# Cross maxima handed over head by head, division and rounding of the outputs on GpSimd, and another order of VectorE's steps

## The reference, cut to what matters

```
x = layernorm(x + self_attention(x))      # 16 heads of 32, 8 key-value heads, rotary angles
x = layernorm(x + cross_attention(x, ctx))# 16 heads of 32, causal, keys and values of ctx @ Wkv
x = layernorm(x + ffn(x))                 # silu(x @ w1.T) * (x @ w2.T) @ w3.T

# self attention: all 4 blocks of 128 keys are among the 8 selected, so no key is masked
scores = q @ k.T / sqrt(32);  probs = softmax(scores);  out = (probs @ v) @ wo
# cross attention: scores = where(lower triangle, scores, lowest float)
# ffn weights go through NF4 and back: scaled = block / max|block| per 64 weights,
# the nearest of 16 steps, times the scaler, which is itself stored as 8 bits about its mean
```

## Time and profile before

| | before |
|---|---|
| median of 3 runs, us | 1255.36 (1251.58 to 1261.95) |
| profiled execution, us | 1259.52 |
| its span, us | 1257.6 |
| mean granted clock of TensorE | 0.935 |
| busy us: TensorE, VectorE, ScalarE, GpSimd | 1063.7, 793.3, 474.3, 396.2 |

### The profile page before, as it was taken

How to read it: one execution, slowest core, us unless ns; L and a number is a source line. 1 busy time by engine, 2 the same in 40 slices (tenths; PEclk the granted TensorE clock), 3 DMA queues, 4 the chain that set the end, 5 groups by cost and what they waited for, 6 DMA issues and landing times.

```text
span 1257.6 us, 17320 instructions
## 1 busy us (share of the span) xinstructions
PE 1063.7 (85%) x6248; PEld 681.6 (54%) x6248; DVE 793.3 (63%) x1628; ACT 474.3 (38%) x582; POOL 396.2 (32%) x427
## 2 busy tenths in 40 slices
PE   6869697888898789898887888878868899999995
PEld 4535244444554435445544555545534688888884
DVE  6676554765677466854876786687585554545444
ACT  3323242463444463453465455455434121212100
POOL 4526743384535634301223222222243600000000
PEclk9769898998998799999898998999897999999998
DMA  5722266355632674363475456457552510202010
GB/s 199 218 54 47 73 164 174 95 145 144 192 96 94 168 204 129 108 131 86 113 193 137 119 136 154 106 133 174 138 129 72 171 51 1 101 1 67 1 67 34
DMA packets 81808, 145.12 MB, mean 115 GB/s; under 512 B 14984, under 2 KB 31728, under 8 KB 81468
## 3 DMA queue, kind: packets, MB, share of 16 engines
q1 hardware_dynamic: 68812, 104.03, 32.1%
q0 software_dynamic: 11888, 39.73, 10.9%
q10 hardware_dynamic: 1024, 0.26, 0.1%
HBM read 78.09 MB, written 23.73 MB: 81 GB/s over the span
## 4 chain that ended last, share of the span: by engine, by line
PE 59%; DVE 20%; ACT 5%; POOL 5%; DMA 5%; issue 4%; SPq 1%; ACTq 0%; DVEq 0%; POOLq 0%
PE att_pv L922 11%; PE att_scores L1134 6%; PE att_pv L1134 6%; PE att_scores L866 6%; PE att_scores_T L1164 6%; PE att_scores_T L854 6%; PE att_scores_T L855 5%; PE att_scores_T L856 5%; PE att_scores_T L898 3%; DVE att_mx L1469 3%; DVE att_scores L1464 3%; ACT att_probs L1290 2%; PE att_scores_T L1024 2%; DMA att_q_stack<-att_m_rows 2%; DVE att_nf_zone L1586 2%
## 5 line engine op out<-in xcount | busy, mean ns | idle before, releaser
L1290 ACT ACTIVATE att_probs<-att_scores_T 128x1024 f32<-128x1024 f32 (+2 forms) x256 | 219.3, 883 | 311.6 <-PE att_scores_T L898 308.5
L866 PE MATMUL att_scores<-att_k_stack,att_q_stack 96*128 96x256 f32 (+1 forms) x504 | 166.2, 413 | 78.6 <-DVE att_mx L1469 49.4
L922 PE MATMUL att_pv<-att_probs,att_v 128*32 128x512 f32 (+3 forms) x1024 | 226.7, 568 | 5.3 <-POOL att_probs L708 4.9
L922 PE MATMUL att_pv<-att_probs,att_ones 128*32 128x512 f32 (+3 forms) x1024 | 226.7, 568 | 0.0
L1469 DVE TENSOR_REDUCE att_mx<-att_scores 128x2 f32<-128x1024 f32 x124 | 151.6, 1223 | 107.5 <-PE att_scores L866 106.6
L1464 DVE CUSTOM_DVE_ANT_0 att_scores<-att_scores,att_cmask 128x128 f32<-128x128 f32 (+3 forms) x256 | 120.9, 511 | 59.6 <-PE att_scores L866 59.0
L866 PEld LDWEIGHTS att_scores<-att_k_stack,att_q_stack 96*128 96x128 f32 x504 | 88.8, 203 | 124.2 <-DVE att_mx L1469 45.7
L898 PE MATMUL att_scores_T<-att_q_stack,att_k_stack 97*128 97x512 f32 (+2 forms) x512 | 146.3, 398 | 11.4 <-DVE att_nf_zone L1600 4.5
L708 POOL TENSOR_SCALAR_AFFINE_SELECT att_probs<-att_probs 128x256 f32<-128x256 f32 x128 | 59.6, 466 | 264.5 <-ACT att_probs L1290 262.3
L898 PEld LDWEIGHTS att_scores_T<-att_q_stack,att_k_stack 97*128 97x128 f32 x512 | 90.9, 201 | 56.7 <-issue 18.0
L922 PEld LDWEIGHTS att_pv<-att_probs,att_v 128*32 128x32 f32 x1024 | 51.9, 116 | 119.0 <-issue 94.8
(11 more groups left out here) (251 smaller groups left out, 2083.0 us busy)
## 6 DMA issues: line engine op xcount, KB each, us to landing
att_q_stack<-att_q_hi SPq DMA_DIRECT2D x128, 128.0 KB, 3.1
att_probs<-nf_x SPq DMA_DIRECT2D x28, 352.0 KB, 3.6
att_nf_home<-nf_reciprocals POOLq DMA_DIRECT2D x48, 176.0 KB, 5.0
att_q_stack<-att_q_lo SPq DMA_DIRECT2D x64, 128.0 KB, 3.6
att_k_stack<-att_k_hi SPq DMA_DIRECT2D x64, 128.0 KB, 3.5
att_nf_home<-nf_x SPq DMA_DIRECT2D x20, 352.0 KB, 3.6
w_nf<-att_nf_zone SPq DMA_DIRECT2D x192, 22.0 KB, 2.6
att_k_stack<-att_k_hi SPq DMA_DIRECT2D x64, 64.0 KB, 2.6
```

The source lines that it names most:

```text
L866: last = T.matmul(sco[:, r, 0:width], qst[0:96, s, r, P * t:P * t + P], kst[0:96, r if crossed(b) else 0, s, 0:width], start=True, stop=True)
L922: last = T.matmul(pv[HD * j:HD * j + HD, sums, q0:S], lhs, pr[:, at:at + S - q0], start=(t == 0), stop=(t == TT - 1))
L1290: A.activation(probs_of(b, r)[:, 1024 * h:1024 * h + w], bank[:, 0:w], ACT.Exp, scale=SCALE).then_inc(st_free, 1)
```

## The change

1. In cross rounds the semaphores between score matmuls and maxima count single heads. TensorE waits for the bank of the head that it is about to write, and VectorE for the head that it is about to read.
2. The division of the outputs by their sums and the rounding to `oh` go from VectorE to GpSimd (`weighed`), ahead of the subtraction there. VectorE keeps the two transposes and the reciprocal (`over_sums`). The last group of a batch is closed in round 0 of the next batch instead of round 1.
3. The first half of a batch's input is rounded in round 7 two batches ahead instead of round 0 of the batch before (`halved`); the second half stays in round 1.
4. The layer norm is split: statistics and Newton iteration (`spread`) at the end of round 2, the scalings of rows 0 and 1 between maxima 0 and 1 of round 3, of rows 2 and 3 behind maxima 1.
5. ScalarE takes two passes (0, 1) in rounds 3 and 4 of self batches 0 to 2, and one elsewhere, where it took three (0, 1, 3) in rounds 3, 4 and 5.
6. Maxima 3 stand ahead of the rounding of rotated queries and keys (`hi_of_raw`) where they stood behind it.
7. The quantisation of the scalers is split over rounds 4 and 5 of batch 0.

```diff
-    return (0, 1, 3) if u < SELF_ROUNDS and b < B - 1 and p in (3, 4, 5) else (0,)
+    return (0, 1) if u < SELF_ROUNDS and b < B - 1 and p in (3, 4) else (0,)
+def halved(b, p):
+    if b == 0 and p < 2:
+        return 1, p
+    if p == NP - 1 and b + 2 < B:
+        return b + 2, 0
+    if p == 1 and b + 1 < B:
+        return b + 1, 1
+    return None
...
-            def lo_of_o(G):
+            def weighed(G):
+                pool.wait_ge(o_over, G + 1)
...
+                pool.tensor_tensor(pvr[:, 0, :], pvr[:, 0, :], turn[:, :], ALU.mult).then_inc(o_div, 1)
+                pool.wait_ge(o_div, G + 1)
+                pool.tensor_copy(oh[:, G % KT, :], pvr[:, 0, :]).then_inc(o_hi, 1)
                 pool.wait_ge(o_hi, G + 1)
                 pool.tensor_tensor(ol[:, G % KT, :], pvr[:, 0, :], oh[:, G % KT, :].bitcast(F32), ALU.subtract).then_inc(o_ok, 1)
...
+                    if p % 2 == 0 and pairs(b, p) > 0:
+                        weighed(pairs(b, p) // 2 - 1)
+                    if halved(b, p):
+                        n, h = halved(b, p)
+                        lo_of_x(n, h)
...
+                n, each = unit_of(b, p, t), crossed(b) and (b, p, t) != (B, 0, 0)
+                if n > 0 and not each:
+                    pe.wait_ge(sc_free, n)
                 for r in range(2):
+                    if each:
+                        pe.wait_ge(sc_free, n - 1 + r)
                     last = T.matmul(sco[:, r, 0:width], qst[0:96, s, r, P * t:P * t + P],
                                     kst[0:96, r if crossed(b) else 0, s, 0:width], start=True, stop=True)
-                last.then_inc(sc_full, 1)
+                    if crossed(b) or r == 1:
+                        last.then_inc(sc_full, 1)
...
                     for r in range(2):
+                        dve.wait_ge(sc_full, unit_of(b, p, t) + r + 1)
+                        V.tensor_tensor_reduce(out=sco[:, r, 0:width], in0=sco[:, r, 0:width], in1=cmask[:, S - width:S],
...
+                                               accum_out=mx[:, p % 2, TT * r + t:TT * r + t + 1]).then_inc(sc_free, 1)
...
-            def normalise(G):
+            def over_sums(G):
                 ch.need()
...
-                ch.tick(V.tensor_tensor(pvr[:, 0, :], pvr[:, 0, :], turn[:, :], ALU.mult))
-                ch.need()
-                V.tensor_copy(oh[:, G % KT, :], pvr[:, 0, :]).then_inc(o_hi, 1)
...
                     if fore:
                         maxima(*fore, 0)
-                    if closing:
-                        sums_of(KT * b - 1)
+                    if p == 3 and b > 0:
+                        scale_rows(range(0, 2), TT - 1)
                     if fore:
                         maxima(*fore, 1)
-                    if closing:
-                        normalise(KT * b - 1)
-                    if p in (2, 4, 6):
+                    if p % 2 == 0 and pairs(b, p) > 0:
                         sums_of(G)
                     if p == 3 and b > 0:
-                        layer_norm(range(TT))
+                        scale_rows(range(2, TT), TT - 1)
...
+                    if fore and not early:
+                        maxima(*fore, 3)
                     for unit in turned_behind(b, p):
                         hi_of_raw(unit)
-                    if fore and not early:
-                        maxima(*fore, 3)
...
+                    if p == 2 and b > 0:
+                        spread(range(TT))
```

More of the change, by code:

```diff
@@ L202, in unit_of @@
     def unit_of(b, p, t):
-        return (pairs(b, p) - 1) * TT + t
+        n, own = (pairs(b, p) - 1) * TT + t, (pairs(B, 0) - 1) * TT
+        return n + max(0, n - own)
     def halves_of(b):
@@ L789, in _ @@
                         pool.wait_ge(k1_ok, 1)
-                    if p == 1 and 0 < b and not crossed(b):
-                        lo_of_o(KT * b - 1)
                     if (b, p) == (B - 1, 3):
@@ L838, in _ @@
                         ffn_convert(k)
-            lo_of_o(KT * NB - 1)
+            weighed(KT * NB - 1)
             for k in range(10, len(PIECES_F)):
@@ L1334, in _ @@
                     exponential(b, p, 2)
-                    if p < 2 and b + 1 < B:
-                        hi_of_x(b + 1, p)
+                    if halved(b, p):
+                        hi_of_x(*halved(b, p))
                     if 0 in mine:
@@ L1504, in layer_norm, with scale_rows @@
                 reciprocal_sqrt(V, ch, mv[:, lo:hi, 1], nwt[:, :, lo:hi], nwi[:, lo:hi])
+            def scale_rows(ts, end):
                 for t in ts:
@@ L1507, in layer_norm @@
                                            ALU.subtract, ALU.mult)
-                    if t < ts[-1]:
+                    if t < end:
                         ch.tick(last)
@@ L1511, in layer_norm @@
                         last.then_inc(ln_ok, 1)
+            def layer_norm(ts):
+                spread(ts)
+                scale_rows(ts, ts[-1])
             def largest(i):
@@ L1627, in _ @@
                     fore = after(b, p, LEAD)
-                    G = KT * b + p // 2 - 1
+                    G = pairs(b, p) // 2 - 1
                     closing = p == 1 and b > 0
@@ L1645, in _ @@
                     if (b, p) == (0, 4):
+                        centre_scalers()
+                    if (b, p) == (0, 5):
                         quantise_scalers()
@@ L1656, in _ @@
                         add_residual(b - 1, 1)
-                    if p in (2, 4, 6):
-                        normalise(G)
+                    if p % 2 == 0 and pairs(b, p) > 0:
+                        over_sums(G)
                     if (b, p) == (0, 2):
```

49 lines of the change are left out of this document (24 added, 25 removed).

## The result

The changed kernel is slower: 1279.13 us median of four runs (1277.81 to 1291.97), against 1258.65 for the kernel before, over its runs beside them. The ratio is 1.0205, with a 95% interval of 1.0107 to 1.0302. I had forecast 1249 with a range of 1232 to 1268, so time and sign are both outside what I expected; R2, the rival that ended slower, named the right place and, with 1267, somewhat over half of the loss. The sign that the prediction gave for being wrong came as well: stalls from C in all self batches too.

What follows compares the result with a forecast made beforehand. TensorE, busy 1063.7 of 1257.6 us, was taken to set the end. The terms -7 - 6.3 + 6.4 - 4.8 + 3.1 + 1.6 + 0.5 sum to -6.5, applied to the 1255.4 median: 1249 us, range 1232 to 1268.

Steps and rivals of the forecast that it cites:

- R2: Rival: statistics ahead of the maxima in round 3, steps stretched by GpSimd, make it slower, about 1267 us; chance .14.
- The sign that the prediction gave for being wrong: Round 3 stalls of C absent (1242 or less) or in all self batches too (1260 or more).
- C: Layer norm statistics moved ahead of maxima 0 of round 3: +6.4 us, bounds -10 and +23.
- A: Cross rounds: maxima handed over head by head hide one head's matmul per real wait, -7 us.
- B: Last pair closed a round earlier, input half made in round 7: projection stalls in rounds 1.1 and 2.1 go, -6.3 us.
- D: Rounds 5 and 6 of batches 1 and 2: fourth maxima ahead of the rotated query's rounding, 2.4 gained each, -4.8 us.
- E: GpSimd multiplies and rounds the outputs instead of VectorE, mostly covered by its waiting: +3.1 us, bounds -5 and +21.
- F and G: Last pair's sums ahead of the third pass in round 0, +1.6 us; later scaler DMAs in batch 0, +0.5 us.
- The cross part of C: Batches 4 to 6, round 3: a 3.9 us stall, net +2.2 each plus 0.6 for a slow stretch, +8.4 us.
- The other half of B: Round 2.1: the other projection wait, 1.8 us, goes with its slow stretch, -3 us.
- R4: Rival: GpSimd blocks VectorE at half of the 32 output pairs, +10.4 instead of +3.1, 1256 to 1257 us; chance .15.
- R1: Rival: freed stalls cascade, 1225 us, 1246 with half the gains, about 1238 where C costs nothing; chance .22.

Runs made afterwards that it cites:

- heads_off: spread_back with cross maxima handed over for both heads at once again; ratio 1.0064 to the kernel before, 14.5 us slower than spread_back.
- heads_only: The kernel before with one edit, cross maxima handed over head by head; ratio 0.9871, 16 us faster than the kernel before.
- spread_back: The changed kernel with the layer norm whole again behind maxima 1 of round 3; ratio 0.9949 to the kernel before.
- spread_only: The kernel before with only the layer norm split, statistics at the end of round 2; ratio 1.0155, 19.5 us slower.
- dve_divides: spread_back with multiplication and rounding of the outputs on VectorE again, at the new places; ratio 0.9911 to the kernel before.
- spread_quiet: The changed kernel, GpSimd starting the rotation of rounds 1.2 and 2.2 only after maxima 0 of round 3; ratio 1.0004 to the kernel before.
- rounding_behind: Changed kernel with round 3 statistics behind maxima 1, scalings behind maxima 2, and q1's rounding behind maxima 1 of round 6; 1234.12 us, ratio 0.9763.

## Why the prediction was wrong, by its own steps

| term | forecast, us | measured | from |
|---|---|---|---|
| A, heads | -7 | -14.5 and -16 | heads_off, heads_only |
| B, closing and input half | -6.3 | +4 in rounds 1: +2.5 in 1.1, -2.8 in 2.1, +4.4 in 4.1, 5.1 and 6.1 | table, traces |
| C, statistics | +6.4 | +28.6 in rounds 3; +32 and +19.5 by ratios | spread_back, spread_only |
| D, maxima before rounding | -4.8 | -2.0, with E's +5.3 in it | table, dve_divides |
| E, division on GpSimd | +3.1 | +4.8, intervals overlap | dve_divides |
| F and G | +2.1 | about +1 | batch 0 128.2 to 126.8; rounds 7 of batches 1, 2 and 0 of batches 2, 3 44.3 to 47.1 |

The rows overlap and are not a sum: D and E meet in the same rounds, and the sizes from ratios carry intervals of 4 us and more to either side.

*C failed, and decided.* The sentence that failed says that in rounds 1.3 and 2.3 the chain is already the cause of the stall (3.10 us), and "becomes one of that size a unit earlier: 0". The three self batches cost 19.7 us (8.6, 6.1, 5.0) of the 28.6. Two things were wrong in it. At its old place the chain stood behind two maxima that had fed TensorE, and met the last two operations of the rotation: it lasted 6.1 us, with steps of 1.45 and 2.26 us (the second in the earlier trace rows), and TensorE had projections to do meanwhile. At the new place it met all three operations and lasted 9.6 us, and TensorE had only the end of a round's weighing to do. I had both figures: a step stretched from 0.17 to 2.26, and GpSimd's rotation of three such operations in a row. I had even costed the same contention in R2, as one stretched step, and given it no place in C. What had to be done was to lay the moved chain over GpSimd's queue at the new place, step by step. In round 3.3 the next sentence failed: the stall of 3.52 us was to shrink by 1, the new stall ahead of maxima 0 is 7.31 us with one caught step of 2.95, and the round grew by 5.0. In round 7.3 it held: -1 forecast, and the round is 1.8 us shorter. What the term lacked is shown by spread_back, spread_only and spread_quiet together: the place costs, and at that place GpSimd makes two thirds of the stall of a round with rotation.

*The cross part of C* was right in mechanism and stall (3.83 us for 3.9). The size was off: +10.7 for batches 4 to 6, where I had 8.4. I had given the slow stretch behind the stall 0.6 of its 2.2 us, and that may be the difference; no run separates it.

*A* was mis-sized by half: the term counts a head's matmul and must count a head's maximum too. *B* took one road from a late landing to TensorE for the only one. The second was hidden in the trace of before: ScalarE's exponential behind the pass ended at 207.78, and TensorE reached only at 209.16 the matmul that waits for it in the changed kernel, because the first road had held it until 205.58. I had seen that VectorE's passes limit the gain to 3.3; with ScalarE's pass in front of an exponential there was none, 33.1 us for 30.5. That is within what round 1.1 varies by. The other half of B came as forecast, -2.8 for -3 in round 2.1. *D* failed in the changed kernel: a stall in front of one unit was moved in front of the next, since the rotation it waits for ends later there, 18.9 us behind the start of round 2.5 instead of 17.7. With the division on VectorE it ends at 16.5, and the four rounds fall by 7.9 us against the kernel before, more than D's 4.8. So what D lost it lost to E, and I had added the two as if they were independent. *E* was right in sign, and its size is near but not settled, as the intervals overlap; R4's rule (every pair is blocked) cost less than feared, and the cross batches gained. The Trainium skill, "SBUF — State Buffer", section "Who interferes with whom", calls the pair of ports shared by the two engines an exclusive lock. The three steps that each end with a GpSimd instruction, and spread_quiet, agree. It bore on C, the term in which I did not use it.

*R2* had sign and place. It said 3.3 us a batch in seven batches; six of them cost 3 to 9, and batch 7 gained 1.8. In R1, "about 1238 where C costs nothing" is 1239.5 by its own terms; nothing hangs on it.

## What to carry to other kernels

A chain of small dependent steps is as long as its neighbours let it be: when it is moved, lay it step by step over the other engine's queue at the new place, and look first whether it then stands ahead of the step that feeds the busiest engine. Moving a wait past one unit only helps if there is enough work ahead of it to cover the wait; here three units (rounding_behind) were enough and one was not. Gains measured one at a time need not add up: an edit that lets an engine start earlier can bring its work beside another engine's, as the division did in round 0.5. Where two engines hand the same buffers back and forth, halving the piece that is handed over shortened the loop on both sides here.

## What the runs showed of the hardware that I had not expected

While GpSimd ran its three 128x1024 tensor operations, VectorE got one blocked instruction through per GpSimd instruction: three steps of four columns took 2.88, 2.23 and 2.19 us instead of 0.17, each ending with an operation of GpSimd. That is not a fixed count: in round 3.3 one step of four columns took 2.95 us and ended at 519.31, behind two subtractions of GpSimd that ended at 519.28. The blocked steps at 375.15, 516.36 and 140.22 began 0.48, 0.43 and 0.70 us before GpSimd's tensor operation and still did not get through; why is not shown. And between executions of one kernel on one chip the time varied by 1 to 2%: 1255.93 to 1274.53 us in 18 of 19 runs of the kernel before, 1281.47 in the other.
